# A state-space layer with routed experts on one core: where the scratch's empty rows are written, and from which queue

## What is computed

```python
x = x + ga * ssm(layernorm(x) * (1 + ca) + sa)
x = x + gb * experts(layernorm(x) * (1 + cb) + sb)

# ssm: x, z, B, C, dt are projections of its input; 512 channels, 16 states
delta = softplus(dt_lin + bdt);  u = silu(conv4(x))
h = exp(delta * A) * h + (delta * u) * B      # scan over the 1024 tokens, per channel and state
y = (h * C).sum(over states)
out = ((y + u * D) * silu(z)) @ Wout.T + bout

# experts: the two largest gate logits, softmax over the two
out = sum over the two of weight * (silu(x @ w0[e]) * (x @ w1[e])) @ wo[e]
```

## Time and profile before

| | us |
|---|---|
| median of 3 runs | 921.65 |
| the profiled execution | 922.18 |
| its span, first to last instruction | 920.4 |
| of the span: VectorE busy | 645.6 |
| GpSimd busy | 504.0 |
| TensorE busy (matmuls) | 738.3 |

### The profile page before, as it was taken

How to read it: one execution, slowest core, us unless ns; L and a number is a source line. 1 busy time by engine, 2 the same in 40 slices (tenths; PEclk the granted TensorE clock), 3 DMA queues, 4 the chain that set the end, 5 groups by cost and what they waited for, 6 DMA issues and landing times.

```text
span 920.4 us, 10283 instructions
## 1 busy us (share of the span) xinstructions
PE 738.3 (80%) x2240; PEld 365.7 (40%) x2241; DVE 645.6 (70%) x878; ACT 322.9 (35%) x359; POOL 504.0 (55%) x263
## 2 busy tenths in 40 slices
PE   5899996777777877878778787875059999999994
PEld 3434342223222322323223233664026666666663
DVE  4467687989999899989989999655314444444442
ACT  1677755453454445434444542011011111111110
POOL 1000014897999999899899999207602222222222
PEclk9999997999999999999899999995569999999998
DMA  9353304656556565655555555752632222222220
GB/s 268 99 149 98 125 26 136 219 182 201 216 195 218 180 221 181 226 172 203 198 198 200 203 219 203 257 200 88 199 112 44 39 42 44 42 42 44 45 39 0
DMA packets 73060, 132.85 MB, mean 144 GB/s; under 512 B 10506, under 2 KB 46666, under 8 KB 72908
## 3 DMA queue, kind: packets, MB, share of 16 engines
q1 hardware_dynamic: 62676, 123.77, 40.2%
q0 software_dynamic: 7152, 8.48, 5.5%
q10 hardware_dynamic: 3208, 0.34, 0.3%
HBM read 93.82 MB, written 35.47 MB: 140 GB/s over the span
## 4 chain that ended last, share of the span: by engine, by line
PE 46%; DMA 15%; POOL 15%; DVE 12%; issue 7%; ACT 4%; ACTq 0%; SPq 0%; POOLq 0%; DVEq 0%
PE PS L651 15%; DMA hT<-C_scratch 13%; PE PS L449 9%; POOL pool L1307 8%; DVE pool L1041 7%; PE PS L667 7%; PE PS L548 6%; PE PS L564 3%; POOL spread L1330 3%; POOL expert_in_scratch L1354 2%; ACT PS L804 2%; PE PS L659 2%; DVE pool L1029 1%; PE PS L530 1%; PE PS L639 1%
## 5 line engine op out<-in xcount | busy, mean ns | idle before, releaser
L1307 POOL TENSOR_TENSOR pool<-pool,hT 128x1024 f32<-128x1024 f32 x128 | 299.9, 2362 | 31.6 <-PE PS L548 24.3
L548 PE MATMUL PS<-pool,ident 128*128 128x512 f32 x512 | 263.4, 639 | 61.1 <-POOL pool L1307 61.0
L1041 DVE TENSOR_TENSOR_SCAN pool<-PS,pool 128x1024 f32<-128x1024 f32 x96 | 215.7, 2274 | 0.6 <-ACT PS L804 0.6
L804 ACT ACTIVATE PS<-pool,negA 128x1024 f32 (+1 forms) x128 | 143.1, 1118 | 201.0 <-DVE pool L1041 200.9
L548 PEld LDWEIGHTS PS<-pool,ident 128*128 128x128 f32 x512 | 97.0, 199 | 171.7 <-POOL pool L1307 92.0
L1373 POOL DMA_INDIRECT out<-uT,ptab x39 | 60.6, 1553 | 184.3 <-DVE uT L1254 182.3
L651 PE MATMUL PS<-pool,uT 128*128 x312 | 142.5, 600 | 0.8 <-ACT uT L865 0.4
L1029 DVE TENSOR_TENSOR pool<-PS,pool 128x1024 f32<-128x1024 f32 x96 | 117.6, 1225 | 21.5 <-ACTq L798 6.7
L530 PE MATMUL PS<-pool 96*128 96x512 bf16 x256 | 81.7, 402 | 36.6 <-DVE pool L1029 35.0
L1228 DVE TENSOR_TENSOR uT<-uT,PS 128x512 f32<-128x512 f32 x39 | 26.9, 689 | 92.7 <-PE PS L651 89.9
L1330 POOL TENSOR_TENSOR spread<-spread,pool 128x1024 f32<-128x1024 f32 x32 | 75.5, 2361 | 27.7 <-DMA hT<-C_scratch 27.7
(11 more groups left out here) (163 smaller groups left out, 697.0 us busy)
## 6 DMA issues: line engine op xcount, KB each, us to landing
hT<-C_scratch SPq DMA_DIRECT2D x128, 512.0 KB
expert_in_scratch<-zrow SPq DMA_DIRECT2D x68, 261.0 KB, 7.6
pool<-in_w SPq DMA_DIRECT2D x16, 512.0 KB, 10.6
uT<-expert_in_scratch SPq DMA_DIRECT2D x39, 130.5 KB, 2.1
Y<-Y SPq DMA_DIRECT2D x32, 128.0 KB, 2.4
C_scratch<-Y SPq DMA_DIRECT2D x8, 512.0 KB, 2.6
Y<-in_wo SPq DMA_DIRECT2D x8, 512.0 KB, 10.6
x_tok<-in_x SPq DMA_DIRECT2D x4, 512.0 KB, 9.1
```

Source lines behind the costliest of these rows:

```text
L548: m = pe.matmul(PS[:, 6 + half, :], ident[:, :], prod[:, k % PR, HF * half:HF * half + HF], start=False, stop=k == DS - 1)
L804: act.activation(pair(2 * (k % 2)).unsqueeze(1), delta[:, bass.ds(g2 * 2 + r, 1), :], ACT.Exp, scale=decay[:, bass.ds(g2 * (2 * DS) + n, 1 ...
L1041: dve.tensor_tensor_scan(hst[:, k % HR, :], pair(2 * (k % 2)), driven, 0.0, ALU.mult, ALU.add).then_inc(scan_done, 1)
L1307: gp.tensor_tensor(prod[:, k % PR, :], hst[:, k % HR, :], crep[:, k % RC, :], ALU.mult).then_inc(prod_done, 1)
```

## The change

The 68 writes leave SyncE's queue and go to GpSimd's. They stand in a loop after the two steps for the layer norm and ahead of the first `du`. GpSimd waits for the four steps on `zrow` first, a wait that SyncE had before. A partition now writes its two rows to neighbouring rows of the scratch, as one piece of 2088 bytes, where it wrote two pieces of 1044 bytes that lay 128 rows apart. All empty rows but for one note are the same, and that note names a token past the last in either order.

```diff
@@ sync
-            def zeros(i):
-                sp.dma_start(xs_dram[bass.ds(i * (ZS * P), ZS * P), :].rearrange("(n p) c -> p n c", p=P),
-                             zrow[:, :].rearrange("p (n c) -> p n c", c=XW)).then_inc(xs_zeroed, 16)
-
             sp.sem_inc(stk_free, 1)
-            sp.wait_ge(zero_rows, 4)
             sp.sem_inc(prod_done, RC)
...
-                        if k % 2 == 0:
-                            zeros((g2 * 2 + r) * 8 + k // 2)
...
-            for i in range(NG * 8, NZ):
-                zeros(i)
@@ gpsimd
+            def zeros(i):
+                gp.dma_start(xs_dram[bass.ds(i * (ZS * P), ZS * P), :].rearrange("(p n) c -> p (n c)", n=ZS),
+                             zrow[:, :]).then_inc(xs_zeroed, 16)
+
+            gp.wait_ge(zero_rows, 4)
+            with gp.Fori(0, NZ) as i:
+                zeros(i)
             gp.wait_ge(z_mm, 1)
             gp.wait_ge(u_done, 2 + 1)
             gp.wait_ge(delta_done, 1)
```

## The result

The change makes the kernel slower. The changed kernel takes 939.59 us, the median of 4 runs (934.26 to 944.34), against 920.72 us for the kernel before (4 runs, 918.29 to 925.3). The ratio is 1.0186, with a 95% interval of 1.0143 to 1.023. The forecast was 916.2 us with a range up to 932.

What follows compares the result with a forecast made beforehand. VectorE and GpSimd, busy 403 and 396 of the scan's 434 us, were taken as near their limit. 922.2 us profiled less 5.5 (0.7 + 4.8), projections at 0, gives 916.7, as median 916.2 us; range 908 to 932.

Steps and rivals of the forecast that it cites:

- The bytes in the projections: Projections: 18.2 MB of writes take 54 us, fit beside 38 us of other traffic into 110 us; cost 0.
- a share near 0.9: Projections: a DMA share near 0.9 in the changed profile, named as a sign that the forecast holds.
- The taps: Projections: doubled landing makes TensorE 2 us late per sequence, absorbed by 2.05 us idle; cost 0, bound 5 us.
- GpSimd's queue: Projections: 68 writes at 1.26 us take 85.7 us, the last issued at 116.5, `du` not late; cost 0.
- slower rival: Projections: writes over 1.58 us each make the first `du` and the scan late; 934.7 us, chance of slower 0.18.
- The rule against the change: Projections: GpSimd can't write descriptors during VectorE's 2-port operations; 5.5 us added to the 85.7, still ending before 138.
- The gain in the scan: Scan: 0.7 us for an earlier second read of C and 4.8 us for late reads, 5.5 us in all.
- nothing comes of it: Rival, scan: reads of C may be late by themselves; gain 0 to 3 us, 918.7 to 921.7, chance 0.33.
- Part 1: Scan: without the writes' issue and bytes on SyncE's queue, reads of C land sooner; gain 5.5 us.
- The largest rival: Scan: late reads set the pace, so VectorE's 14.4 us wait for the drive goes, and 0.7; 906.6 us, chance 0.12.
- What the prediction said would show it wrong: First L1029 moves, writes over 1.58 us apart, TensorE's projections longer, or scan shortened by under 3 or over 9 us.
- The gain above 5.5 us: Scan: if reads of C use 8 nearly always busy engines, the gain lies between 5.5 us and the upper bound.

Runs made afterwards that it cites:

- e1: The kernel before, with 68 more GpSimd DMAs of 128 pieces of 20 bytes to an unread side tensor in the projections: 928.06 us, ratio 0.9964.
- e4: The changed kernel, with at most two of GpSimd's writes in flight and the loop written out: 950.88 us, ratio 1.0236.
- e5: The changed kernel, with at most four of GpSimd's writes in flight: 929.04 us, ratio 1.008.
- e11: The changed kernel once more, unaltered, beside the kernel before in another session: 943.53 us, ratio 1.0187.
- e8: The changed kernel, with GpSimd writing two pieces of 1044 bytes for each partition, 256 a DMA: 947.51 us, ratio 1.0277.
- e9: The kernel before, with 26 writes by GpSimd behind the first `du`, 42 by SyncE as single pieces in the scan's last six chunks: 921.31 us, ratio 0.9982.
- e2: The changed kernel, plus a SyncE DMA of 256 pieces of 20 bytes to a side tensor after every second read of C: 959.56 us, ratio 1.0341.

## Why the prediction was wrong

Point by point, by its own steps.

- **The bytes in the projections: the step that failed.** The prediction put 54 us of writes and 38 us of other traffic into 110 us, found that they fit, and priced what they may delay, the taps, at 0 with a bound of 5 us. The runs showed 21.8 and 25.9 us in its place. The size of the bytes was right: in the changed profile GpSimd's queue fills 46.1% of the 110 us from 31 to 141, 51 us:

```profile
q0 software_dynamic: 5440, 18.18, 46.1%
q1 hardware_dynamic: 3840, 11.21, 34.9%
```

  But a sum over a stretch says nothing of when. The writes come as fast as GpSimd can issue them, and by the prediction's own prices, 54 us of bytes in 85.7 us of issuing, they would have filled 0.63 of the engines, on top of 0.45 that were in use, so more than all. It even named a share near 0.9 as a sign that it was right, and didn't ask what that does to a tap. At the real pace, 0.85 us a write, the writes alone ask for 0.88 (51 us in 58). e1 shows that it is the bytes, e4 and e5 that less of them in flight costs the projections less.
- **The taps.** They were named as what could be late, with a bound of 5 us, on the thought that a landing doubles and an idle time of 2.05 us takes it up. The landing went to 3.9 us at the median but to 9.8 at most, and SyncE's issue of a tap to as much as 2.53 us, so the later taps and the stores behind them on the same queue were late, too. TensorE waited 15.2 us for taps and ran at half its clock or little more behind each of the three waits, and VectorE waited 10.6 us for a store of C. The second sequence, priced like the first, lost nothing: 12.15 us for its taps in both kernels. The price was 21.8 and 25.9 us in the two profiles.
- **GpSimd's queue.** Priced at 1.26 us a write from the indirect DMAs of the earlier trace rows, measured 0.54 + 0.31 = 0.85. The conclusion, that `du` isn't late, held; its slower rival needed over 1.58 us a write. That mechanism is real (e4, 1.98 us), but it isn't what happened. The kernel was slower by another way than the rival that stood for it.
- **The rule against the change.** The Trainium skill, SBUF — State Buffer, "SBUF: two separate sides", lets VectorE's 2-port operations lock GpSimd out of its descriptors. The traces agree with it in part, and the price is small. All writes of the changed kernel, and then two rows of e4, where GpSimd's write begins just before VectorE's L955 (L963 before):

```profile
L1286 POOL DMA_DIRECT2D expert_in_scratch<-zrow x68: 539/539/789, 31.4 to 88.6; - x68
```

```profile
73.85 0.90 POOL L1287 DMA_DIRECT2D expert_in_scratch<-zrow  x1 [1.33 <-DMA expert_in_scratch<-zrow]
73.94 0.68 DVE L955 TENSOR_SCALAR pool<-pool 128x1024 f32<-128x1024 f32 x1
```

  L955 is taken here for such an operation, since at 0.68 us it is nearly twice as fast as one on two tensors of the same size (1.22). The write takes 0.90 us instead of 0.54 and ends at 74.75, 0.13 us behind it. In e1 five of the 68 DMAs are held up so, each beside such an operation. In the changed kernel three such operations run beside the writes (41.29, 47.19 and 88.44). Only the last write is held up, from 0.54 to 0.61 us; the writes at 41.74 and 47.70, which begin while one runs, take 0.54. The 5.5 us that the prediction allowed for it were never reached.
- **The gain in the scan.** Forecast 5.5 us: 0.7 for the issue at the start and 4.8 for late reads. In the changed kernel's first profile GpSimd waited in the scan as follows, and no line names a read of C:

```profile
POOL spread L1328 <- ACT spread L801: 29.7, 5, 27.7
POOL pool L1305 <- PE PS L539: 13.4, 14, 1.6
POOL pool L1305 <- DVE pool L1032: 4.3, 2, 2.7
```

  But the second profile of the same kernel (e11) has 3 such waits behind the first read, 3.5 us, and other kernels without a write in the scan have more than the 6 and 4.8 us of before: e4 7 and 9.7 us (its last write is issued at 165.5), e8 7 and 11.3 us. e1, with all writes in the scan, has 10 and 10.1 us. So reads are late with and without the writes beside them, as the rival "nothing comes of it" had it ("the reads may simply be late by themselves"). That the writes made them late, the mechanism of Part 1, isn't shown; only the first two chunks of e9 point that way. At equal clock the scan is 2.1 us shorter in one pair of profiles (e11), and e9 gains nothing that can be told: the term of 4.8 us was worth at most about 2. The largest rival fares no better: VectorE's wait for the drive, 14.4 us before, is 6.5 us in the first profile of the changed kernel and 15.8 in the second.
- **What the prediction said would show it wrong** did: the first product moved, the projections got longer, and in the first profile the scan was shortened by more than 9 us, in the second by less than 3.

## What to carry to other kernels

Before DMAs are moved to a stretch, compare the pace at which they will be issued with what the DMA engines have free at that moment, not their sum with the stretch's length: an engine that has nothing else to do issues them in one burst. Ask which transfers on other queues have no time to spare there, since all queues share the engines. Fewer DMAs in flight protect the others and take the time from the engine that issues. A transfer that the chain gives 13% says little of a gain: here the writes were taken from beside it, and the scan got 2 us shorter at equal clock, if at all.

## What the runs showed of the hardware

- A plain DMA of 128 pieces costs GpSimd 0.54 us and 0.31 us to the next in a loop, an indirect one of 128 rows 0.96 and 0.30; with 256 pieces the plain one costs 0.74 us (e8). Beside VectorE's TENSOR_SCALAR of 0.68 us a plain one took up to 0.98 us (e1).
- While GpSimd's writes filled the engines, the issue of a tap on SyncE itself took up to 2.53 us (1.24 at most before), and four stores of B 7.23 us (2.30 before). Pressure on the engines reached back into another engine's instruction queue.
- Writes of 261 KB followed each other after 1.98 us with two in flight (e4, landing after 3.3 us at the median), after 1.31 us with four (e5), and after 0.85 us with no bound, that is at about 135, 204 and 314 GB/s (an estimate from size and pace).
- After idle times of 6.97 and 5.01 us TensorE's granted clock was 0.50, and four matmuls took 3.78 and 3.77 us, which is what eight took at 1.00.
- 64 DMAs of 256 pieces of 20 bytes between the reads of C (e2) went with a ratio of 1.0341 where the changed kernel has 1.0186.
- The Trainium skill, DMA: Bandwidth & Descriptors, "Why a DMA increments its semaphore by 16 and not by 1", gives the reads of C 8 engines. The scan of the changed kernel has hardly more than reads of C and a DMA share of 0.47, the time of 7.5 of 16 engines, which fits it and doesn't show it; single engines aren't in the rows. The gain above 5.5 us that the prediction drew from this rule didn't come.
